# A two-layer transformer on one core: the first batch's stages in a written-out order, with its small set-up work moved between engines

## The reference

```
# layer 0
h = layernorm(x) * (1 + ca) + sa
score = (h Wq)(h Wk)^T / sqrt(32), causal; zeros replaced by the lowest float
x = x + ga * softmax(score) @ (h Wvdown Wvup)
h = layernorm(x) * (1 + cb) + sb
probs = softmax(h Wg + bg); e = argmax(probs) % 8
x = x + gb * relu(h We[e] + be[e]) * max(probs)
# layer 1
h = layernorm(x) * (1 + ca) + sa
x = x + ga * (attention with 16 heads of 8 channels (h) Wout^T + bout)
h = layernorm(x) * (1 + cb) + sb
x = x + gb * ((h W1[b]^T + b1[b]) W2[b]^T + b2[b])
```

## Time and profile before

| | us |
|---|---|
| median of 3 runs | 1827.22 |
| lowest and highest | 1825.13, 1828.02 |
| the profiled execution's own time | 1829.32 |
| span of that execution, first to last instruction | 1828.0 |
| mean granted clock of TensorE | 0.969 of full |

### The profile page before, as it was taken

How to read it: one execution, slowest core, us unless ns; L and a number is a source line. 1 busy time by engine, 2 the same in 40 slices (tenths; PEclk the granted TensorE clock), 3 DMA queues, 4 the chain that set the end, 5 groups by cost and what they waited for, 6 DMA issues and landing times.

```text
span 1828.0 us, 54376 instructions
## 1 busy us (share of the span) xinstructions
PE 1658.2 (91%) x23051; PEld 653.3 (36%) x23051; DVE 1503.9 (82%) x2301; ACT 1389.1 (76%) x1960; POOL 730.3 (40%) x1173
## 2 busy tenths in 40 slices
PE   5657899999999999999999999999999999999994
PEld 2532343334333343334333343333433343322222
DVE  5547988899888988898888988899888987999942
ACT  3433578887798877887788877987788877887882
POOL 3321345335554275434554265434654354102011
PEclk9976799999999999999999999999999999999996
DMA  2130111112210312112211222103111122102101
GB/s 69 49 95 25 57 57 58 30 40 72 81 56 25 85 54 86 33 46 73 72 56 34 60 57 93 46 23 96 59 57 34 39 71 84 51 24 57 34 17 41
DMA packets 97458, 100.32 MB, mean 55 GB/s; under 512 B 11136, under 2 KB 81600, under 8 KB 97216
## 3 DMA queue, kind: packets, MB, share of 16 engines
q1 hardware_dynamic: 95476, 95.08, 17.6%
q10 hardware_dynamic: 1740, 1.77, 0.3%
HBM read 61.30 MB, written 34.73 MB: 53 GB/s over the span
## 4 chain that ended last, share of the span: by engine, by line
PE 62%; DVE 15%; ACT 13%; issue 6%; POOL 4%; DMA 1%; ACTq 0%; SPq 0%; POOLq 0%
PE pv_psum L777 21%; PE side_psum L542 14%; PE buffer L761 11%; PE buffer L751 10%; DVE row_max L1230 8%; ACT p L971 7%; PE buffer L542 2%; PE side_psum L630 2%; PE side_psum L597 1%; POOL xn_attn L1264 1%; ACT o_sb L977 1%; DVE s L1109 1%; DVE st_f L1024 1%; ACT s L889 1%; ACT s L882 1%
## 5 line engine op out<-in xcount | busy, mean ns | idle before, releaser
L1230 DVE TENSOR_REDUCE row_max<-buffer 128x2 f32<-128x1024 f32 x1024 | 1235.9, 1219 | 180.8 <-PE buffer L751 170.3
L971 ACT ACTIVATE p<-buffer 128x1024 f32<-128x1024 f32 x1024 | 1046.8, 1027 | 203.5 <-PE buffer L761 186.4
L777 PE MATMUL pv_psum<-p,v 128*9 128x256 f32 x8192 | 583.5, 381 | 6.6 <-ACT o_sb L977 5.9
L751 PE MATMUL buffer<-k_ops,q_ops 48*128 48x512 bf16 x2048 | 397.3, 385 | 32.8 <-ACT p L971 12.1
L761 PE MATMUL buffer<-q_ops,k_ops 51*128 51x512 bf16 x2048 | 400.8, 388 | 12.8 <-DVE row_max L1230 11.8
L777 PEld LDWEIGHTS pv_psum<-p,v 128*9 128x9 f32 x8192 | 149.9, 89 | 316.7 <-issue 234.2
L761 PEld LDWEIGHTS buffer<-q_ops,k_ops 51*128 51x128 bf16 x2048 | 98.2, 93 | 379.8 <-issue 234.8
L1359 POOL TENSOR_TENSOR hm<-masks,hT_f 128x1024 f32<-128x1024 bf16 x56 | 120.1, 2150 | 112.5 <-PE side_psum L542 112.5
L751 PEld LDWEIGHTS buffer<-k_ops,q_ops 48*128 48x128 bf16 x2048 | 99.4, 94 | 135.2 <-ACT p L971 104.8
L1372 POOL TENSOR_SCALAR nm_parts<-nm 128x16 bf16<-128x16 f32 x64 | 16.3, 254 | 285.8 <-DVE nm L1179 285.3
L542 PE MATMUL side_psum<-we,hm 128*32 128x128 f32 x3648 | 120.9, 274 | 0.9 <-DVE hm L1173 0.9
(11 more groups left out here) (269 smaller groups left out, 1650.0 us busy)
## 6 DMA issues: line engine op xcount, KB each, us to landing
masks<-masks_rows SPq DMA_DIRECT2D x16, 1024.0 KB, 5.7
q_ops<-products SPq DMA_DIRECT2D x128, 96.0 KB
k_ops<-products SPq DMA_DIRECT2D x126, 96.0 KB
products<-q_parts SPq DMA_DIRECT2D x16, 384.0 KB, 2.6
products<-k_parts SPq DMA_DIRECT2D x14, 384.0 KB, 2.6
attention<-o_sb SPq DMA_DIRECT2D x256, 18.0 KB
x<-in_L_attn_inputs SPq DMA_DIRECT2D x8, 512.0 KB, 4.0
products<-q_parts SPq DMA_DIRECT2D x16, 256.0 KB, 2.9
```

Source lines behind the costliest of these rows:

```text
L751: m = e.matmul(buffer[:, hh, :], q_ops[rows_of(hh, K_MAX), slot, of, i * P:(i + 1) * P], k_ops[rows_of(hh, K_MAX), slot, of, halves(half)[ ...
L777: m = e.matmul(pv_psum[q:q + VW, half * QUARTER:(half + 1) * QUARTER], v1[b % 2][:, kb, 2 * hp + hh, :], p_sb[n % KEPT][:, hh, part * QUAR ...
L971: e.activation(p_sb[n % KEPT][:, :, :], unit("exp", n)[0][:, :, :], ACT.Exp).then_inc(S["exp_done"], 1)
L1230: e.tensor_reduce(mx[pair % 2][:, :, i, half], unit("max", n)[0][:, :, :], axis=AX.X, op=ALU.max).then_inc(S["max_done"], 1)
```

## The change

The assumed times are replaced by a list written out by hand (`ALONE`), with the same 185 stages in another order; two gaps of the plan of the later batches are one shorter; and set-up work is moved:

- the ones of `k_ops` are written by ScalarE, as one copy over the whole tile of a constant whose bits are two bf16 ones (`two_ones`), after its first exponential; the memsets of GpSimd go
- Wq and Wk are loaded ahead of the modulation weights under a semaphore of their own, and transposed and multiplied ahead of the modulation
- the gate products of TensorE move from before `g0 0 0` to before the stage `gates 0`, into the bank `pv_psum`; VectorE's five gate instructions, with what stood around them, move to the same stage, and the second half's `apply` moves behind the modulation copy
- `residual` of batch 0 is on VectorE
- ScalarE issues one of the three stores of each key half of batch 0, SyncE the other two; SyncE fetches all of the first pair's operands, and x of batches 2 and 3 after them

```diff
-           (0, ("gating", half, 0)), (2, ("onehot", half)), (0, ("gating", half, 1)), (3, ("onehotT", half)), (1, ("over_gating", half)),
+           (0, ("gating", half, 0)), (2, ("onehot", half)), (0, ("gating", half, 1)), (2, ("onehotT", half)), (1, ("over_gating", half)),
...
-    return out + [(2, ("v1", half))]
+    return out + [(1, ("v1", half))]
...
+GATE_AT, WEIGHTS_AT = ("gates", 0), (("scores", 0, 4, 0), ("scores", 0, 6, 0))
+
+ALONE = """
+apply 0 0 1, apply 0 0 0, channels 0 0 0, stats 0 0 1 0, g0 0 0, channels 0 0 1, stats 0 0 0 0, gates 0, g0 0 1, scores 0 0 0, stats 0 0 1 1, v0 0,
+scores 0 1 0, softmax 0 0, exp0 0 0, stats 0 0 0 1, softmax 0 1, transpose_p 0 0 0, later 0, scores 0 2 0, exp0 0 1, times_v 0 0, transpose_p 0 1 0,
+softmax 0 2, scores 0 3 0, exp0 0 2, times_v 0 1, transpose_p 0 2 0, softmax 0 3, scores 0 4 0, exp0 0 3, sums0 0 0, scores 0 4 1, transpose_p 0 3 0,
+transpose_p 0 3 1, scores 0 5 0, exp0 0 4, softmax 0 4, scores 0 5 1, times_v 0 2, times_v 0 3, transpose_p 0 4 0, transpose_p 0 4 1, softmax 0 5,
+up 0 0, scores 0 6 0, exp0 0 5, stats 0 1 0 0, scores 0 6 1, times_v 0 4, stats 0 1 0 1, transpose_p 0 5 0, softmax 0 6, scores 0 7 0,
+transpose_p 0 5 1, exp0 0 6, scores 0 7 1, times_v 0 5, stats 1 0 0 0, transpose_p 0 6 0, channels 0 1 0, apply 0 1 0, softmax 0 7,
+transpose_p 0 6 1, exp0 0 7, sums0 0 1, wg 0 0, times_v 0 6, stats 1 0 0 1, transpose_p 0 7 0, top 0 0 0, stats 1 0 1 0, index 0 0 0,
+transpose_p 0 7 1, top 0 0 1, stats 1 0 1 1, times_v 0 7, index 0 0 1, onehot 0 0, gating 0 0 0, up 0 1, gating 0 0 1, stats 0 1 1 0, apply 1 0 0,
+stats 0 1 1 1, onehotT 0 0, masks_out 0 0, over_gating 0 0, channels 0 1 1, apply 0 1 1, hm 0 0, apply 1 0 1, channels 1 0 0, wg 0 1, top 0 1 0,
+top 0 1 1, g0 1 0, index 0 1 0, channels 1 0 1, index 0 1 1, hm 0 1, gating 0 1 0, moe_a 0 0, g0 1 1, onehotT 0 1, gating 0 1 1, onehot 0 1,
+masks_load 0 0, hm 0 2, hm 0 3, masks_out 0 1, over_gating 0 1, moe 0 0, moe_a 0 1, moe 0 1, masks_load 0 1, moe_a 0 2, v0 1, moe 0 2, moe_a 0 3,
+moe 0 3, gates 1, residual 0 0, hm 0 4, stats 0 2 0 0, scores 1 0 0, hm 0 5, stats 0 2 0 1, moe_a 0 4, softmax 1 0, moe 0 4, apply 0 2 0, hm 0 6,
+exp0 1 0, channels 0 2 0, moe_a 0 5, qk1 0 0 0, later 1, moe 0 5, hm 0 7, parts 0 0 0, moe_a 0 6, qk1 0 1 0, moe 0 6, scores 1 1 0,
+transpose_p 1 0 0, parts 0 1 0, moe_a 0 7, moe 0 7, softmax 1 1, exp0 1 1, residual 0 1, v1 0 0, stats 0 2 1 0, times_v 1 0, stats 0 2 1 1,
+scores 1 2 0, channels 0 2 1, transpose_p 1 1 0, qk1 0 0 1, apply 0 2 1, softmax 1 2, parts 0 0 1, qk1 0 1 1, scores 1 3 0, v1 0 1, exp0 1 2,
+parts 0 1 1, transpose_p 1 2 0, times_v 1 1, sums0 1 0, exp0 1 3, scores 1 4 0, scores 1 4 1, transpose_p 1 3 0, transpose_p 1 3 1, softmax 1 3,
+softmax 1 4, times_v 1 2, scores 1 5 0, exp0 1 4, scores 1 5 1, transpose_p 1 4 0, transpose_p 1 4 1, softmax 1 5"""
...
-    first = sorted(times, key=times.get)
+    first += [stage for h, stage in sorted(ahead, key=lambda some: some[0])]
...
+    two_ones = sb("two_ones", [P, 1])
...
-    def store_parts(queue, b, w, half):
+    def store_parts(queue, b, w, half, some=slice(None)):
 
         cols = halves(half)[1]
-        for r0, r1, part in PART_RUNS[w]:
+        for r0, r1, part in PART_RUNS[w][some]:
...
+        pe.wait_ge(S["in_c"], 48)
+        pe.wait_ge(S["in_qk"], 32)
+        for j in range(2):
+            m = e.transpose(psum[3][0:D0, j * C:(j + 1) * C], wqk0[:, j, :], ident)
+        m.then_inc(S["w0_transposed"], 1)
+        pe.wait_ge(S["wqkT"], 1)
+        e.matmul(psum[2][:, 0:C], wqkT[:, 0, :], wqkT[:, 1, :], start=True, stop=True).then_inc(S["a0_mm"], 1)
...
-        def weights():
-            for j in range(2):
-                m = e.transpose(psum[6][0:D0, j * C:(j + 1) * C], wqk0[:, j, :], ident)
-            m.then_inc(S["w0_transposed"], 1)
-            gate_view = psum[4][0:B, :].rearrange("p (j c) -> p j c", c=C)
+        def gate_products():
+            gate_view = pv_psum[0:B, :].rearrange("p (j c) -> p j c", c=C)
             for l in range(2):
                 for j, six in enumerate((2, 5)):
                     m = e.matmul(gate_view[:, 2 * l + j, :], cT[:, l, :], wmod[l][:, six, :], start=True, stop=True)
             m.then_inc(S["gate_mm"], 1)
-            pe.wait_ge(S["wqkT"], 1)
-            e.matmul(psum[2][:, 0:C], wqkT[:, 0, :], wqkT[:, 1, :], start=True, stop=True).then_inc(S["a0_mm"], 1)
...
             pe.wait_ge(S["in_rest"], 15 * 16)
+            pe.wait_ge(S["gate"], 1)
...
-        early = {("g0", 0, 0): weights, WEIGHTS_AT[0]: weights_natural, WEIGHTS_AT[1]: weights_late}
+        early = {GATE_AT: gate_products, WEIGHTS_AT[0]: weights_natural, WEIGHTS_AT[1]: weights_late}
...
+        act.wait_ge(S["two_ones"], 1)
+        e.copy(k_ops[:, :, :, :].rearrange("p s g n -> p (s g n)").bitcast(F32), two_ones[:, 0:1].broadcast_to([P, SLOTS * GROUP * N // 2])).then_inc(S["operands_set"], 2)
+        act.wait_ge(S["w0_transposed"], 1)
+        e.copy(wqkT[:, :, :], psum[3][0:D0, 0:2 * C].rearrange("p (j c) -> p j c", c=C)).then_inc(S["wqkT"], 1)
+        act.wait_ge(S["a0_mm"], 1)
+        e.mul(a0[:, :], psum[2][:, 0:C], D0 ** -0.5).then_inc(S["a0"], 1)
...
-                store_parts(e, b, w, half)
+                store_parts(e, b, w, half, slice(0, 1))
...
-        act.wait_ge(S["operands_set"], 2)
-        act.wait_ge(S["parts1"], 16 * STORES)
-        fetch_operands(e, 0, 1)
...
+        e.memset(two_ones[:, :], TWO_ONES).then_inc(S["two_ones"], 1)
...
-        apply(0, 0, 1)
...
+        apply(0, 0, 1)
+
+        def gate_rows():
+            e.tensor_copy(ident_bf[:, :], ident).then_inc(S["ident_bf"], 1)
+            dve.wait_ge(S["gate_mm"], 1)
+            gate_view = pv_psum[0:B, :].rearrange("p (j c) -> p j c", c=C)
...
+        def residual(b, q):
+            if b:
+                return
+            tiles, x = halves(q)[0], xs[b % 4]
+            dve.wait_ge(S["side_act"], side["moe", b, 4 * q + 3].emptied)
+            after(e.tensor_tensor(xn_f[:, tiles, :], xn_f[:, tiles, :], gates[b % 3][:, 1, :].unsqueeze(1).broadcast_to([P, 4, C]), op=ALU.mult))
+            e.tensor_tensor(x[:, tiles, :], x[:, tiles, :], xn_f[:, tiles, :], op=ALU.add).then_inc(S[f"x2_{q}"], 1)
...
-        pool.wait_ge(S["zero_rows"], 4)
-        for hh in range(2):
-            m = e.memset(k_ops[ROW_HALF * hh + 32:ROW_HALF * (hh + 1), :, :, :], 1.0)
-            m.then_inc(S["operands_set"], 1)
-            pool.wait_ge(S["operands_set"], hh + 1)
...
+        for dst, src in ((wqk0[:, 0, :], Wq0), (wqk0[:, 1, :], Wk0)):
+            e.dma_start(dst, src).then_inc(S["in_qk"], 16)
         for dst, src in ((wmod[0][:, :, :], wmod0.rearrange("k (j c) -> k j c", c=C)),
-                         (wmod[1][:, :, :], wmod1.rearrange("k (j c) -> k j c", c=C)),
-                         (wvd[:, :], Wvdown), (wqk0[:, 0, :], Wq0), (wqk0[:, 1, :], Wk0)):
+                         (wmod[1][:, :, :], wmod1.rearrange("k (j c) -> k j c", c=C)), (wvd[:, :], Wvdown)):
...
-            if (b, w) == (0, 1):
-                return
             sp.wait_ge(S[f"split{w}_{half}"], b + 1)
             if b >= 2:
                 for g in range((b - 1) * GROUPS - GROUPS, (b - 1) * GROUPS):
                     sp.wait_ge(*operands(g))
-            store_parts(e, b, w, half)
+            store_parts(e, b, w, half, slice(1, None) if (b, w) == (0, 1) else slice(None))
...
-            for w in range(2 if g else 1):
+            for w in range(2):
...
+        load_operands(0)
         load_x(2)
         load_x(3)
-        load_operands(0)
```

More of the change, by code:

```diff
@@ L166, in lay_out @@
     return at
-PACE = {"stats": 0.9, "apply": 1.6, "channels": 1.2, "wg": 1.6, "top": 1.0, "index": 0.9, "gating": 0.3, "onehot": 0.6, "onehotT": 1.2,
-        "over_gating": 0.5, "masks_out": 0.1, "masks_load": 2.2, "hm": 1.2, "moe_a": 0.6, "moe": 0.6, "residual": 1.5, "qk1": 1.2, "parts": 0.6,
-        "v1": 1.0, "gates": 1.5, "g0": 1.5, "v0": 1.5, "later": 1.0, "scores": 0.8, "softmax": 1.2, "exp0": 0.9, "sums0": 0.0, "transpose_p": 0.9, "times_v": 1.0, "up": 1.6}
-AFTER_MASKS = 3.0
-TILES_FROM, TILE_PACE, VALUES_FROM = 22.0, 2.6, 31.0
@@ L177 @@
-WEIGHTS_AT = (("scores", 0, 4, 0), ("scores", 0, 6, 0))
-SECOND_FROM, SECOND_PACE, ALONE_UNTIL = 40.0, 1.6, 0
-def alone_times():
-    times = {("stats", 0, 0, half, part): 0 for half in range(HALVES) for part in range(2)}
-    times.update({("apply", 0, 0, half): 0 for half in range(HALVES)})
-    for n, stage in enumerate((("channels", 0, 0, 0), ("g0", 0, 0), ("channels", 0, 0, 1), ("gates", 0), ("g0", 0, 1))):
-        times[stage] = 12.0 + 2 * n
-    times.update({("v0", 0): TILES_FROM + 2.2, ("later", 0): TILES_FROM + 3.5})
-    for i in range(T):
-        t = TILES_FROM + TILE_PACE * i
-        for c in range(len(chunks(i))):
-            times["scores", 0, i, c] = t + 0.5 * c
-        times["softmax", 0, i] = t + 1.5
-        times["exp0", 0, i] = t + 2.8
-        for c in range(len(blocks(i))):
```

(30 more changed lines are left out.)

47 lines of the change are left out of this document (24 added, 23 removed).

## The result

The median of the changed kernel is 1803.2 us (four executions, 1801.2 to 1804.2) against 1827.5 for the kernel before on the same chip: ratio 0.9869, 95% interval 0.9855 to 0.9884. It is 24 us faster; 14.7 were forecast, and the time lies 0.8 us under the range. The profiled execution took 1803.95 us, its span is 1802.6, so in the two profiled executions the difference is 25.4 (the one before took 1829.3). I account for that one.

What follows compares the result with a forecast made beforehand. Stage order bounds the first 147 us, where no engine is full; VectorE, then TensorE, bound the rest. Parts A to F sum to -14.7 us, taking 1829.3 to 1814.6 (median 1812.5); range 1804 to 1821.

Steps and rivals of the forecast that it cites:

- part F: Plan of the later batches: moved stages add no work, so 0, allowing 0.7 us either way per batch.
- The third rival: Slower, chance 0.05: moved steady-batch stages come too soon for their masks and hold score units; 1833 at 3.5 us each.
- Part E: Last key split to first score unit: SyncE shares stores and fetches keys at once, so operands land sooner; -6.5 us.
- Part D: First to second residual statistics: residual on VectorE -1.2, fewer ScalarE stores -1.1, splits some 1.7 sooner; -4.0 us.
- the splits that come sooner: Between the residuals: `qk1 0 0 0` ahead of two TensorE stages brings the splits some 1.7 us sooner.
- Masks: First batch, before tile 3's experts: masks about 2 us sooner, `hm 0 0` ahead of `wg`; costed at nothing.
- Parts A, B, C: Up to the first gates -2.0 us; one-hot for first batch's masks earlier -0.7; first half's residual on VectorE -1.5.
- the first (operands no sooner): Before the first score unit: shared transfers make part E cost 1.42 us instead of saving 6.5; 1820.4, chance 0.15.
- The second (a higher clock): Before 147 us: less waiting keeps TensorE nearer full clock, eight more fast stages, -7 us; 1805.5, chance 0.13.

Runs made afterwards that it cites:

- the four kernels with the same code: The changed kernel with both gaps back, either gap back, or the loads of x ahead of the first fetches: 1808.9, 1804.8, 1806.8, 1808.7 us.

## Why the prediction came out as it did

The sign and the places held, and the mechanisms of the lone stretch; the sum was 10.7 us too small. 4.8 of them are part F, 5.9 lie ahead of the first score unit; without either of the two the time would have stood inside the range. The terms that were mis-sized:

- **Part F, the step that failed** (forecast 0, measured 4.8). I reasoned from "No work is added" and allowed the idle time 0.7 either way for each batch. Six batches gained 0.4 to 0.8 us each, 3.8 in all; the other 1.0 is the piece up to the first `wff`, which varies by itself. The two lines alone gave 4.4 in the kernel before and cost 5.7 when undone. The third rival had the right object, stages that meet a wait, and the wrong sign. The trace of before shows where to look: TensorE waits 0.33 us for hT twice in every batch, with no value products between score and `g0` there. How the waits would balance it does not show, since covering these two brought a new one of 0.65.
- **Part E** (6.5, measured 8.5). From the split to SyncE's key fetch I had 6.05 us, measured are 4.0 (117.38 to 121.39); from there to the first unit 5.1 and 5.1. I let the store stand 1.3 us behind an exp; in the trace ScalarE sat idle 1.68 us waiting for the split, since the exp had been done, and stores were issued at once (0.46 for one) and landed in 3.56.
- **Part D** (4.0, measured 5.9). Two of its three steps hold in size: from the split to the statistics it is 2.4 us less, forecast 2.3, and the copy of tile 7 waits for 0.46 of issuing, not for 1.61. The third, the splits that come sooner, was to give 1.7 and gave 3.6. In the four kernels with the same code it gives 1.9 to 2.1, and D as a whole 4.3 to 4.6. So the term was nearly right, and the rest is luck with TensorE's clock, which the sum left out. In the changed kernel's profile the 64 products at 87.43 took 3.64 us, TensorE was then idle for only 2.00, and the next 32 took 1.05; with both gaps back the 64 products at 86.90 took 1.95, it sat idle for 3.69, and the next 32 took 1.62. In the trace of before it was idle for 7.23, and the 64 products at 99.91 took 3.63.
- **Masks** (0, measured 1.4; 0.9 to 1.4 with the kernels of the same code). I let TensorE's queue end last there. With the old order and all else as changed the piece is as long as before (24.3 us), so the order is the cause. Which exchange it is, and whether it is `hm 0 0` ahead of `wg` (at 72.59), is not shown.
- **Parts A, B, C** (4.2, measured 4.6) hold with their steps: hT at 13.65 (forecast 13.9), gates stage at 22.60 (23.1), a wait of 3.25 (3.15), residual in two instructions of 0.69, and `hm 0 4` between it and the statistics. That the sum of A is so near is luck: it is worth 0.6 to 3.1 us, by the execution.

Of the rivals, the first (operands no sooner) fell: the keys' issue back on ScalarE costs 9.9 us. The second (a higher clock) held in part, some 1.5 of its 7 us, in part D and in this execution. The third fell. The singly undone parts, order 4.6, residual 5.8, keys 9.9, ones 3.4, gaps 5.7 us, sum to 29, and to 35 with the place of the loads, 5.5; the gain is 24. By the ratios, which set each kernel against the one before on its own chip, they are 5.1, 4.9, 9.3, 4.6, 6.6 and 7.1. That they overlap, each letting another wait end last, is likely but not shown; the error of each cost and the executions' own spread also go into the excess.

## What to carry to other kernels

A plan that adds no work can still be worth its moves: before pricing one at nothing, list the small waits of the bounding engine in a steady period and ask which of them would get cover, and which new ones would come. For an in-order engine that issues DMAs, price what the issue stands behind and what stands behind it: here the first was 5.3 us, against 1.8 of slower landing. A saved wait ahead of a chain of matrix stages can also buy their clock, and a wait behind them can take it back. And before reading a difference of 1 to 3 us out of two traces, look at the same piece in kernels that run the same code there.
